# Post-LN attention and gated FFN on eight cores: statistics of the third layer norm taken chunk by chunk inside the w_d projection, its inputs loaded and cast earlier

## Chip, cores, metric

One Trainium2 chip, all 8 cores. Each core runs the same program on its own tokens; there is no exchange between cores. The metric is the time on the device, in microseconds, of the slowest core.

## The reference

What matters of it, for x of shape (4, 4096, 1024), 4 heads of 256:

```python
h = layer_norm(x, ln1_g, ln1_b)
q, k, v = heads(h @ wq), heads(h @ wk), heads(h @ wv)
attn = softmax(q*s, -1) @ (softmax(k*s, -2)^T v)       # linear attention
x1 = x + attn @ wo + bo
h = layer_norm(x1, ln2_g, ln2_b)
x2 = x1 + gelu(h @ w_ff1 + b_ff1) @ w_ff2 + b_ff2      # hidden 4096
u = x + (x2 @ w_d + b_d)                               # outer residual
x3 = layernorm(u)                                      # "ln3" in the kernel
z = (silu(x3 @ wg^T) * (x3 @ wu^T)) @ wd^T             # hidden 3072, weights /127
y = layernorm(x3 + z)                                  # "ln4" in the kernel
```

## The kernel before

Activations lie transposed: features on the 128 partitions in 8 chunks (`CH`), tokens along the free axis in tiles of 512 (`NT`). A core owns 2048 tokens, four tiles, and reads the other 2048 of its batch entry only for k and v. The program has two blocks, PA (ln1, k and v over 8 tiles, then q, then the small matrices of the attention) and PB (everything else). PB goes stage by stage over the four tiles: attention output, four quarters of the first FFN (`qq`, L807 on: 256 matmuls up with gelu on ACT, 256 matmuls down that DVE adds to the fp32 residual `R1`), then the stage of w_d (L943 to L987), then three rounds of the gated FFN (`r`, L1035 on), with ln4 and the output in the last.

Every engine carries out its instructions in the order in which `b.op` records them, and an instruction with a wait (`engine.wait_ge`, L84) holds all that is behind it on that engine. So the order of the Python code is the order of the work. `DmaQ` (L111) keeps two semaphores per queue: transfer k waits until transfer k-2 of the same queue has landed. `gpQ` is issued by POOL, `syQ` by SP.

The w_d stage, for each tile t:

- `est.acquire()` and `load_x` (L217) bring the tile of x, 2 MB, into a half of `estR` by SP. The first two of these wait for the last matmul of the first FFN (`q3b_done`).
- Eight ACT casts (L950) copy the fp32 tile of `R1` to bf16 `shad` (even t) or `shad2` (odd t, printed as shad_51). These lie in `Dr`, over the weights of the last up quarter, and so also wait for `q3a_done`.
- `rows()` and `bcs()` of the tile before (t-1): ACT and DVE turn the sums in PSUM bank `lnS` into mean and reciprocal deviation (L654 to L670), two matmuls spread them over 128 partitions (L676, L680).
- For each of eight output chunks m: eight matmuls (L963) with w_d in `slotD1`, and one DVE instruction (L973) that adds bias and x and writes `R1`. Three PSUM banks (`rot5`) rotate. w_d is loaded by POOL in four pieces of 256 columns (`gds`, L903), all of which wait for `q3b_done`; chunk m needs piece m//2.
- After m == 3, `l3_apply(t-1)`: eight DVE subtractions (L924), eight POOL products (L928) and eight ACT casts to `h2x` (L932).
- After the eight chunks, `stats()` of this tile: for each chunk an ACT cast to bf16 (L634), an ACT square (L636), and one matmul with a column of ones for each (L638, L642). The two buffers in `sbb` alternate between chunks, and all of it waits for the last L973 of the tile (`extra_stat_waits`).

The rows and the apply of tile 3 come in the first round of the gated FFN. `mk_ln` (L615) serves ln2 and ln4 too; there the statistics run on ACT, or on POOL where `cast_eng` is "gpsimd".

Of the kernel before, what the change touches and what calls it, by code (L numbers as in the profile page):

```python
# [125 lines left out]
def build_nc(debug=False, phases=99):  # L126
# [488 lines left out]
    def mk_ln(t, xsrc_c, kind, extra_stat_waits=(), cast_eng="scalar"):  # L615
# [6 lines left out]

        def stats():
            for c in range(CH):
                xb = sbb[:, (c % 2) * 512:(c % 2) * 512 + 512]
                xq_ = sbb[:, 1024 + (c % 2) * 512:1024 + (c % 2) * 512 + 512]
                vw = list(extra_stat_waits) + [("te", ln_state[f"sbb_free{c % 2}"])]
                if cast_eng == "gpsimd":
                    ve1 = b.op("gpsimd", lambda e, c=c, xb=xb: e.tensor_copy(
                        xb, xsrc_c(c)), waits=vw, inc="gp2")  # L630
                    ve2 = b.op("gpsimd", lambda e, xb=xb, xq_=xq_: e.tensor_mul(  # L631
                        xq_, xb, xb), inc="gp2")
                else:
                    ve1 = b.op("scalar", lambda e, c=c, xb=xb: e.activation(  # L634
                        xb, xsrc_c(c), AF.Identity), waits=vw, inc="se")
                    ve2 = b.op("scalar", lambda e, xb=xb, xq_=xq_: e.activation(  # L636
                        xq_, xb, AF.Square), inc="se")
                b.op("tensor", lambda e, xb=xb, c=c: e.matmul(  # L638
                    lnS["ap"][0:1, :], onescol, xb, start=(c == 0), stop=False,
                    skip_group_check=True),  # L640
                    waits=[(cast_sem, ve1)] + (Pool.w(lnS) if c == 0 else []))
                te = b.op("tensor", lambda e, xq_=xq_, c=c: e.matmul(  # L642
                    lnS["ap"][32:33, :], onescol, xq_, start=(c == 0), stop=False,
                    skip_group_check=True), waits=[(cast_sem, ve2)], inc="te")
# [554 lines left out]
```

How the kernel before makes its waits and increments, by code:

```python
        def run(engine, _w=tuple(w), _fn=fn, _s=semh, _k=inck):  # L82
            for sh, v in _w:
                engine.wait_ge(sh, v)
            inst = _fn(engine)
            if _s is not None:
                inst.then_inc(_s, _k)
# [38 lines left out]
def build_nc(debug=False, phases=99):  # L126
# [469 lines left out]
    def tap(name, src_handle, shape, dtype):  # L596
        th = nc.dram_tensor(name, shape, dtype, kind="ExternalOutput")
        b.begin("tap")
        ov = syQ.dma(lambda e: e.dma_start(th.ap(), src_handle[:, :]))
        b.op("sync", lambda e, ov=ov: e.wait_ge(b.sem[ov[0]], ov[1]))
        b.end()
# [517 lines left out]
                xsrc = lambda c, t=t: R1[:, c * NOWN + t * NT:  # L1119
                                         c * NOWN + (t + 1) * NT]
                L4[t] = mk_ln(t, xsrc, "ln4",
                              extra_stat_waits=[("ve", down_evac[t])])
                L4[t]["stats"]()
        wd_free[r % 2] = b.cnt["te"]
    L4[3]["rows"]()
    L4[3]["bcs"]()
    l4_apply(3)
    kf = syQ.k
    b.op("sync", lambda e, v=16 * ((kf + 1) // 2): e.wait_ge(b.sem["syA"], v))
    b.op("sync", lambda e, v=16 * (kf // 2): e.wait_ge(b.sem["syB"], v))
    b.end()
```

## Time and profile before

| | us |
|---|---|
| Time, median of 2 runs (2002.55 to 2003.36) | 2002.96 |
| The profiled execution's own time | 2016.04 |
| Its span on the slowest core, core 1 | 2014.5 |
| Spans of the eight cores | 1989.4 to 2014.5 |
| PE busy on core 1 | 1665.6 (83%) |
| DVE, ACT, POOL busy | 549.2, 517.9, 121.1 |

The time is that of the slowest core. All rows of the profile below are of core 1 in the one profiled execution; their times count from the start of its span. That execution took 13 us more than the median of the others. L-numbers are lines of the kernel before.

### The profile page before, as it was taken

The page shows a single profiled execution, that of the slowest core. Times are in us where ns is not written, and L with a number is a line of the kernel's source. Part 1 is how long each engine was busy: PE and PEld are TensorE (multiplying, and loading weights), DVE is VectorE, ACT ScalarE, POOL GpSimd, SP SyncE. Part 2 cuts the span into 40 slices and gives each one's busy share as a digit, 9 for nine tenths or more (in the row PEclk, how much of TensorE's full clock was granted, in tenths as well). Part 3 has the DMA queues.
Part 4 walks back from the last instruction along what each step waited for, and adds up shares of the span by engine and source line. Part 5 has one row for each costly group of instructions (what it writes and reads, how often), then busy time and mean ns, then how long its engine had stood idle before and what let it go on. Part 6 is the DMA issues. An engine that isn't in the chain of part 4 may idle for free.

```text
span 2014.5 us, 20572 instructions; the slowest of 8 cores (1989.4 to 2014.5 us)
## 1 busy us (share of the span) xinstructions
PE 1665.6 (83%) x7096; PEld 686.7 (34%) x7096; DVE 549.2 (27%) x840; ACT 517.9 (26%) x806; POOL 121.1 (6%) x124
## 2 busy tenths in 40 slices
PE   1489999898677767999999994567999999999774
PEld 0133333343222222444444441112344444444121
DVE  1633333311212442211213041222223213312223
ACT  1232333322232343122120312544210110011422
POOL 0000000000000042000000000111100000000113
PEclk9987777898797777999999997667899999999666
DMA  9311111020027050222211007101003003000112
GB/s 186 70 42 42 43 42 42 1 42 1 0 48 182 22 84 0 42 42 42 42 42 42 1 1 167 42 1 42 1 1 125 1 1 126 1 0 1 42 42 84
DMA packets 47636, 89.58 MB, mean 44 GB/s; under 512 B 1328, under 2 KB 5552, under 8 KB 47536
## 3 DMA queue, kind: packets, MB, share of 16 engines
q1 hardware_dynamic: 30896, 61.01, 9.3%
q0 software_dynamic: 16640, 27.26, 8.4%
q8 instruction: 60, 0.98, 0.2%
q14 instruction: 40, 0.33, 0.1%
HBM read 107.14 MB, written 8.39 MB: 57 GB/s over the span
## 4 chain that ended last, share of the span: by engine, by line
PE 50%; ACT 8%; DVE 4%; POOL 4%; DMA 3%; issue 2%; ACTq 0%; POOLq 0%; DVEq 0%; SPq 0%
PE pb L867 11%; PE pb L841 10%; PE pb L1051 8%; PE pb L1061 8%; PE pb L1104 8%; ACT sbb L636 3%; ACT sbb L634 3%; PE pb L769 2%; PE pb L963 2%; POOL R L928 2%; DMA estR<-xkv 2%; DMA slotD<-wdd 1%; DVE R L1013 1%; POOL sbb L631 1%; ACT shad L950 1%
## 5 line engine op out<-in xcount | busy, mean ns | idle before, releaser
L1051 PE MATMUL pb<-h2x,W 128*128 128x512 bf16 x768 | 186.1, 386 | 3.4 <-ACT slbt L1070 3.4
L1104 PE MATMUL pb<-Dr,wslotE 128*128 128x512 bf16 x768 | 177.0, 394 | 9.2 <-DVE R L1111 9.2
L1061 PE MATMUL pb<-h2x,W 128*128 128x512 bf16 x768 | 183.1, 381 | 0.0
L848 ACT ACTIVATE Gq<-pb,pv 128x512 bf16<-128x512 f32 x128 | 88.1, 689 | 312.0 <-PE pb L841 311.2
L1070 ACT ACTIVATE slbt<-pb 128x512 bf16<-128x512 f32 x96 | 57.4, 598 | 369.0 <-PE pb L1051 365.7
L1075 DVE SCALAR_TENSOR_TENSOR Dr<-slbt,pb 128x512 bf16<-128x512 bf16 x96 | 66.0, 688 | 287.4 <-PE pb L1061 260.0
L418 PE MATMUL pb<-W,h 128*128 128x512 bf16 x512 | 141.8, 428 | 0.0
L882 DVE TENSOR_TENSOR R<-R,pb 128x512 f32<-128x512 f32 x96 | 66.0, 688 | 265.5 <-PE pb L867 265.5
L434 PE MATMUL pb<-slotD,h 128*128 128x512 bf16 x512 | 135.9, 414 | 0.0
L841 PE MATMUL pb<-h2x,W 128*128 128x512 bf16 x512 | 121.0, 401 | 7.3 <-ACT Gq L848 6.0
L1104 PEld LDWEIGHTS pb<-Dr,wslotE 128*128 128x128 bf16 x768 | 76.9, 101 | 107.8 <-issue 23.6
L841 PE MATMUL pb<-h2x,slotD 128*128 128x512 bf16 x512 | 110.8, 379 | 0.0
L867 PE MATMUL pb<-Gq,slotD 128*128 128x512 bf16 x512 | 110.8, 379 | 0.0
L867 PE MATMUL pb<-Gq,W 128*128 128x512 bf16 x512 | 110.8, 379 | 0.0
L1051 PEld LDWEIGHTS pb<-h2x,W 128*128 128x128 bf16 x768 | 75.9, 99 | 97.5 <-issue 9.8
L1061 PEld LDWEIGHTS pb<-h2x,W 128*128 128x128 bf16 x768 | 75.7, 99 | 92.4 <-issue 3.2
L638 PE MATMUL pb<-sbb,cb 128*1 128x512 bf16 x96 | 53.4, 558 | 52.3 <-ACT sbb L634 32.3
L1111 DVE TENSOR_TENSOR R<-R,pb 128x512 f32<-128x512 f32 x96 | 66.0, 687 | 111.3 <-PE pb L1104 110.3
L963 PE MATMUL pb<-shad,slotD 128*128 128x512 bf16 x256 | 67.9, 431 | 29.0 <-DMA slotD<-wdd 19.8
L634 ACT ACTIVATE sbb<-R 128x512 bf16<-128x512 f32 x80 | 50.5, 631 | 155.4 <-DVE R L1111 77.3
L434 PEld LDWEIGHTS pb<-slotD,h 128*128 128x128 bf16 x512 | 53.6, 105 | 72.2 <-issue 48.2
L418 PEld LDWEIGHTS pb<-W,h 128*128 128x128 bf16 x512 | 52.9, 107 | 73.3 <-issue 52.9
(95 smaller groups left out, 1489.1 us busy)
## 6 DMA issues: line engine op xcount, KB each, us to landing
xq<-xkv SPq DMA_DIRECT2D x8, 2048.0 KB, 10.2
estR<-xkv SPq DMA_DIRECT2D x32, 256.0 KB, 3.1
W<-wff POOLq DMA_DIRECT2D x4, 2048.0 KB, 18.9
slotD<-wff POOLq DMA_DIRECT2D x4, 2048.0 KB, 16.4
estR<-xkv SPq DMA_DIRECT2D x4, 2048.0 KB, 11.5
y<-xq SPq DMA_DIRECT2D x4, 2048.0 KB, 6.9
W<-wgT SPq DMA_DIRECT2D x3, 2048.0 KB, 9.8
W<-wuT SPq DMA_DIRECT2D x3, 2048.0 KB, 15.2
```

Source lines behind the costliest of these rows:

```text
L418: b.op("tensor", lambda e, kc=kc, half=half, n0=n0, bk=bk: e.matmul(bk["ap"][:, :], h1[:, kc * N + n0: kc * N + n0 + 128], W1[:, kc * 1024 ...
L434: b.op("tensor", lambda e, kc=kc, half=half, n0=n0, bv=bv: e.matmul(bv["ap"][:, :], h1[:, kc * N + n0: kc * N + n0 + 128], slotD1[:, kc * ...
L634: ve1 = b.op("scalar", lambda e, c=c, xb=xb: e.activation(xb, xsrc_c(c), AF.Identity), waits=vw, inc="se")
L841: b.op("tensor", lambda e, jj=jj, kc=kc, t=t, s1=s1, bk=bk: e.matmul(bk["ap"][:, :], s1[:, kc * 1024 + jj * 128: kc * 1024 + (jj + 1) * 12 ...
L848: se = b.op("scalar", lambda e, jj=jj, t=t, qq=qq, bk=bk: e.activation(Gq[:, jj * NOWN + t * NT: jj * NOWN + (t + 1) * NT], bk["ap"][:, :] ...
L867: b.op("tensor", lambda e, m=m, jc=jc, t=t, s2=s2, bk=bk: e.matmul(bk["ap"][:, :], s2[:, jc * 1024 + m * 128: jc * 1024 + (m + 1) * 128], ...
L882: ve = b.op("vector", lambda e, m=m, t=t, bk=bk: e.tensor_add(R1[:, m * NOWN + t * NT: m * NOWN + (t + 1) * NT], R1[:, m * NOWN + t * NT: ...
L963: b.op("tensor", lambda e, m=m, kc=kc, bk=bk, sh=sh: e.matmul(bk["ap"][:, :], slotD1[:, kc * 1024 + m * 128: kc * 1024 + (m + 1) * 128], s ...
L1051: b.op("tensor", lambda e, hc=hc, kc=kc, t=t, bA=bA: e.matmul(bA["ap"][:, :], W0[:, kc * 1024 + hc * 128: kc * 1024 + (hc + 1) * 128], h2x ...
L1061: b.op("tensor", lambda e, hc=hc, kc=kc, t=t, bB=bB: e.matmul(bB["ap"][:, :], W1[:, kc * 1024 + hc * 128: kc * 1024 + (hc + 1) * 128], h2x ...
L1075: e.scalar_tensor_tensor(Ftn[:, hc * NOWN + t * NT: hc * NOWN + (t + 1) * NT], sl, S127, bB["ap"][:, :], ALU.mult, ALU.mult),
L1104: b.op("tensor", lambda e, m=m, hc=hc, t=t, wds=wds, bk=bk: e.matmul(bk["ap"][:, :], wds[:, hc * 1024 + m * 128: hc * 1024 + (m + 1) * 128 ...
```

## The change

Five edits.

1. In PA the load of wq is issued third instead of first, behind wk and wv.
2. The statistics of ln3 are no longer one block behind a tile. `stats_c(c)` handles one chunk. For tiles 0 to 2 it is recorded right behind the DVE instruction that writes this chunk of `R1`, and waits for it; for tile 3 all eight still stand behind the tile. The cast goes to POOL for even chunks, to ACT for chunks 1 and 5, to DVE for 3 and 7; the square is a DVE product of the bf16 copy with itself.
3. The bf16 copies of tiles 0 and 1 are made in the last down quarter of the first FFN, each chunk right after DVE has written it. Those of tiles 2 and 3 stay at the head of their tile.
4. Piece q of w_d waits for the last down matmul of tile 3 that reads its columns (chunk 2q+1), not for the end of the quarter.
5. `bcs(t-1)` moves from the head of the tile to before m == 2, `l3_apply(t-1)` from behind m == 3 to behind m == 4.

```diff
-    gq = load_w(W0, wq_d, D, CH)
     gk = load_w(W1, wk_d, D, CH)
     gv = load_w(slotD1, wv_d, D, CH)
+    gq = load_w(W0, wq_d, D, CH)
...
+        def stats_c(c, xw=()):
+            xb = sbb[:, (c % 2) * 512:(c % 2) * 512 + 512]
+            xq_ = sbb[:, 1024 + (c % 2) * 512:1024 + (c % 2) * 512 + 512]
+            vw = (list(extra_stat_waits) + list(xw)
+                  + [("te", ln_state[f"sbb_free{c % 2}"])])
+            if cast_eng == "p5":
+                ce = ("gpsimd" if c % 2 == 0
+                      else ("scalar" if c in (1, 5) else "vector"))
+            else:
+                ce = cast_eng
+            if ce == "gpsimd":
+                e1 = ("gp2", b.op("gpsimd", lambda e, c=c, xb=xb: e.tensor_copy(
+                    xb, xsrc_c(c)), waits=vw, inc="gp2"))
...
+            if cast_eng == "p5":
+                e2 = ("ve", b.op("vector", lambda e, xb=xb, xq_=xq_: e.tensor_mul(
+                    xq_, xb, xb), waits=[e1], inc="ve"))
...
+            b.op("tensor", lambda e, xb=xb, c=c: e.matmul(
+                lnS["ap"][0:1, :], onescol, xb, start=(c == 0), stop=False,
+                skip_group_check=True),
+                waits=[e1] + (Pool.w(lnS) if c == 0 else []))
+            te = b.op("tensor", lambda e, xq_=xq_, c=c: e.matmul(
+                lnS["ap"][32:33, :], onescol, xq_, start=(c == 0), stop=False,
+                skip_group_check=True), waits=[e2], inc="te")
...
                 if qq == 3:
                     r1_done[t] = b.cnt["ve"]
+                    if t < 2:
+                        sh_ = shad if t % 2 == 0 else shad2
+                        b.op("scalar", lambda e, m=m, t=t, sh_=sh_: e.activation(
+                            sh_[:, m * NT:(m + 1) * NT],
+                            R1[:, m * NOWN + t * NT: m * NOWN + (t + 1) * NT],
+                            AF.Identity),
+                            waits=[("ve", ve), ("te", q3a_done[0])], inc="se")
...
+                    if t == 3:
+                        q3b_m_te[m] = b.cnt["te"]
...
         ap3(wdd_d, q * 256, [[D, 128], [128 * D, CH], [1, 256]])),
-        waits=[("te", q3b_done[0])]) for q in range(4)]
+        waits=[("te", q3b_m_te[2 * q + 1])]) for q in range(4)]
...
+        L3.append(mk_ln(t, xsrc, "ln3", cast_eng="p5"))
+        if t >= 2:
...
         if t >= 1:
             L3[t - 1]["rows"]()
-            L3[t - 1]["bcs"]()
         for m in range(CH):
+            if m == 2 and t >= 1:
+                L3[t - 1]["bcs"]()
             bk = rot5.acquire()
...
             Pool.rel(bk, "ve", ve)
-            if m == 3 and t >= 1:
+            if t < 3:
+                L3[t]["stats_c"](m, xw=[("ve", ve)])
+            if m == 4 and t >= 1:
                 l3_apply(t - 1)
...
-        L3.append(mk_ln(t, xsrc, "ln3", extra_stat_waits=[("ve", u_evac[t])]))
-        L3[t]["stats"]()
+        if t == 3:
+            for c in range(CH):
+                L3[3]["stats_c"](c, xw=[("ve", u_evac[3])])
```

The order of PE's instructions around the start of tile 1 of the w_d stage, in the kernel before (slotD_49 holds w_d, sbb the statistics' operands, rowb the mean and deviation):

```order
L638 MATMUL pb<-sbb,cb 1x512
L642 MATMUL pb<-sbb,cb 1x512
L676 MATMUL pb<-rowb,cb 128x512
L680 MATMUL pb<-rowb,cb 128x512
L963 MATMUL pb<-shad_51,slotD_49 128x512 x64
L638 MATMUL pb<-sbb,cb 1x512
```

The same place now:

```order
L1002 MATMUL pb<-shad_51,slotD_49 128x512 x8
L651 MATMUL pb<-sbb,cb 1x512
L655 MATMUL pb<-sbb,cb 1x512
L1002 MATMUL pb<-shad_51,slotD_49 128x512 x8
L651 MATMUL pb<-sbb,cb 1x512
L655 MATMUL pb<-sbb,cb 1x512
L694 MATMUL pb<-rowb,cb 128x512
L698 MATMUL pb<-rowb,cb 128x512
L1002 MATMUL pb<-shad_51,slotD_49 128x512 x8
```

A tile's 64 matmuls stood together; now two statistics matmuls stand between every group of eight and the next, and the two spreading matmuls stand behind the second group.

ACT over tile 1 before (shad the bf16 copy of a tile, rsgb the spread deviation, h2x the normalised tile):

```order
L950 ACTIVATE shad_51<-R_43 128x512 x8
L654 ACTIVATE rowb<-pb 1x512
L667 ACTIVATE pb<-pb,pv 1x512
L670 ACTIVATE rowb<-pb 1x512
L919 ACTIVATE rsgb<-pb 128x512
L932 ACTIVATE h2x<-R_43 128x512 x8
L634 ACTIVATE sbb<-R_43 128x512
```

ACT over tile 1 now:

```order
L672 ACTIVATE rowb<-pb 1x512
L685 ACTIVATE pb<-pb,pv 1x512
L688 ACTIVATE rowb<-pb 1x512
L640 ACTIVATE sbb<-R_43 128x512
L951 ACTIVATE rsgb<-pb 128x512
L964 ACTIVATE h2x<-R_43 128x512 x8
L640 ACTIVATE sbb<-R_43 128x512
L985 ACTIVATE shad<-R_43 128x512 x8
```

The second L640 is the statistics cast of chunk 5; it stands behind the eight h2x casts of the tile before. The copy for tile 2 (L985) now stands ahead of the end of tile 1.

DVE in tile 1 now, from its fifth chunk on (R_43 is `R1`; L956 are the subtractions of the apply):

```order
L1012 SCALAR_TENSOR_TENSOR R_43<-pb,pv,estR 128x512
L643 TENSOR_TENSOR sbb<-sbb 128x512
L956 TENSOR_TENSOR R_43<-R_43,pb 128x512 x8
L1012 SCALAR_TENSOR_TENSOR R_43<-pb,pv,estR 128x512
L643 TENSOR_TENSOR sbb<-sbb 128x512
```

Before, it read

```order
L973 SCALAR_TENSOR_TENSOR R_43<-pb,pv,estR 128x512 x4
L924 TENSOR_TENSOR R_43<-R_43,pb 128x512 x8
L973 SCALAR_TENSOR_TENSOR R_43<-pb,pv,estR 128x512 x4
```

Each chunk's DVE instruction is now followed by the square of its chunk, and the subtractions stand one chunk later.

## Rows read from the trace of the kernel before

**Rows 1.** Busy time by window: w_d stage, tile 0's statistics; PEclk is the granted clock.

```profile
core 1: us, PE busy (x) PEld busy (x) DVE busy (x) ACT busy (x) POOL busy (x), PEclk, DMA share, GB/s
...
1207.82:1390.00 182.18, 107.19 (x327) 32.68 (x328) 45.33 (x63) 79.25 (x125) 31.29 (x28) 0.69 0.27 70
...
1243.10:1256.25 13.15, 8.70 (x16) 1.26 (x16) 0.75 (x1) 10.73 (x17) 0.00 (x0) 0.65 0.45 161
```

**Rows 2.** Timeline, start of PA: start, duration, engine, line, operation, idle time before.

```profile
26.52 0.88 POOL L223 DMA_DIRECT2D slotD<-wv  x1 [23.02 <-DMA W<-wq]
...
86.79 3.42 PE L418 MATMUL pb<-W,h 128*128 128x512 bf16 x8
```

**Rows 3.** DMA issues: count, size each, median us from issue to landing.

```profile
slotD<-wv POOLq DMA_DIRECT2D x1, 2048.0 KB, 34.1
```

**Rows 4.** Timeline, start of the w_d stage.

```profile
1207.94 81.49 SPq L217 DMA_DIRECT2D estR<-xkv  x4
...
1208.41 1.75 POOL L903 DMA_DIRECT2D slotD<-wdd  x2 [220.14 <-PE pb L867]
1227.35 4.89 PE L963 MATMUL pb<-shad,slotD 128*128 128x512 bf16 x16 [19.54 <-DMA slotD<-wdd]
...
1230.69 0.75 DVE L973 SCALAR_TENSOR_TENSOR R<-pb,pv,estR 128x512 f32<-128x512 f32 x1 [22.02 <-PE pb L963]
```

**Rows 5.** Issue to landing of L217's loads: at 1205 to 1240 us, then all.

```profile
DMA to landing us min/median/max: 14.4/18.4/22.4
DMA to landing us min/median/max: 8.6/10.2/47.8
```

**Rows 6.** Timeline, from the end of tile 0 to the start of tile 1.

```profile
1244.04 0.63 ACT L634 ACTIVATE sbb<-R 128x512 bf16<-128x512 f32 x1 [70.97 <-DVE R L973]
...
1244.82 0.38 PE L638 MATMUL pb<-sbb,cb 128*1 128x512 bf16 x1 [1.85 <-ACT sbb L634]
...
1255.62 5.69 ACT L950 ACTIVATE shad<-R 128x512 bf16<-128x512 f32 x8
...
1266.92 0.58 PE L680 MATMUL pb<-rowb,cb 1*128 1x512 bf16 x1 [4.21 <-ACT rowb L670]
1267.43 13.97 PE L963 MATMUL pb<-shad,slotD 128*128 128x512 bf16 x56
```

**Rows 7.** Timeline, the apply of tile 0 within tile 1.

```profile
1277.25 6.23 DVE L924 TENSOR_TENSOR R<-R,pb 128x512 f32<-128x512 f32 x8
1278.09 10.25 POOL L928 TENSOR_TENSOR R<-R,rsgb 128x512 f32<-128x512 f32 x8 [44.36 <-DVE R L924]
...
1284.49 3.52 PE L963 MATMUL pb<-shad,slotD 128*128 128x512 bf16 x8 [3.09 <-DVE R L973]
...
1288.18 0.75 DVE L973 SCALAR_TENSOR_TENSOR R<-pb,pv,estR 128x512 f32<-128x512 f32 x1 [2.13 <-PE pb L963]
1288.49 0.63 ACT L932 ACTIVATE h2x<-R 128x512 bf16<-128x512 f32 x1 [0.67 <-POOL R L928]
```

**Rows 8.** Duration min/median/max in ns, first and last start, by line.

```profile
L330 DVE CAST sbb<-xq x64: 426/427/428, 32.6 to 367.1; 128x512 bf16<-128x512 f32 x64
L397 DVE TENSOR_SCALAR h<-h,pv x64: 352/353/355, 55.7 to 408.9; 128x512 bf16<-128x512 bf16 x64
L629 POOL CAST sbb<-R x16: 609/610/630, 707.1 to 766.0; 128x512 bf16<-128x512 f32 x16
```

**Rows 9.** Timeline in PA: a statistics matmul, a group of eight, its ACT reader.

```profile
105.33 0.38 PE L339 MATMUL pb<-sbb,cb 128*1 128x512 bf16 x1 [0.22 <-ACT sbb L332]
105.63 1.90 PE L418 MATMUL pb<-W,h 128*128 128x512 bf16 x8
...
107.69 0.60 ACT L426 ACTIVATE ebf<-pb 128x512 bf16<-128x512 f32 x1 [2.50 <-PE pb L418]
```

**Rows 10.** Timeline, the first statistics cast of tile 3.

```profile
1377.62 0.63 ACT L634 ACTIVATE sbb<-R 128x512 bf16<-128x512 f32 x1
```

**Rows 11.** Chain that ended last: start, us, what; first matmuls of the gated FFN.

```profile
1389.83 3.53 PE pb L1051 x8
```

More of the change, by code:

```diff
@@ L623, in stats @@
         def stats():
             for c in range(CH):
[L625 to L644, printed above, removed]
@@ L645, in stats @@
-                ln_state[f"sbb_free{c % 2}"] = te
-            ch["stat_done"] = b.cnt["te"]
+                stats_c(c)
         def rows():
@@ L687, in mk_ln @@
         ch["stats"] = stats
+        ch["stats_c"] = stats_c
         ch["rows"] = rows
@@ L803, in build_nc @@
     r1_done = [0, 0, 0, 0]
+    shv01 = [0, 0]
+    q3b_m_te = [0] * CH
     q2_done = [0, 0]
@@ L947, in build_nc @@
         syv = load_x(th, toff, t * NT, waits=Pool.w(slot))
-        shv = 0
-        for c in range(CH):
-            shv = b.op("scalar", lambda e, c=c, t=t, sh=sh: e.activation(
-                sh[:, c * NT:(c + 1) * NT],
-                R1[:, c * NOWN + t * NT: c * NOWN + (t + 1) * NT], AF.Identity),
-                waits=[("te", shad_free[t % 2]), ("ve", r1_done[t]),
-                       ("te", q3a_done[0])], inc="se")
+        xsrc = lambda c, t=t: R1[:, c * NOWN + t * NT: c * NOWN + (t + 1) * NT]
+        L3.append(mk_ln(t, xsrc, "ln3", cast_eng="p5"))
+        if t >= 2:
+            shv = 0
+            for c in range(CH):
+                shv = b.op("scalar", lambda e, c=c, t=t, sh=sh: e.activation(
+                    sh[:, c * NT:(c + 1) * NT],
+                    R1[:, c * NOWN + t * NT: c * NOWN + (t + 1) * NT],
+                    AF.Identity),
+                    waits=[("te", shad_free[t % 2]), ("ve", r1_done[t])],
+                    inc="se")
+        else:
+            shv = shv01[t]
         if t >= 1:
             L3[t - 1]["rows"]()
-            L3[t - 1]["bcs"]()
         for m in range(CH):
+            if m == 2 and t >= 1:
+                L3[t - 1]["bcs"]()
             bk = rot5.acquire()
@@ L982, in build_nc @@
         Pool.rel(slot, "ve", u_evac[t])
-        xsrc = lambda c, t=t: R1[:, c * NOWN + t * NT: c * NOWN + (t + 1) * NT]
-        L3.append(mk_ln(t, xsrc, "ln3", extra_stat_waits=[("ve", u_evac[t])]))
-        L3[t]["stats"]()
+        if t == 3:
+            for c in range(CH):
+                L3[3]["stats_c"](c, xw=[("ve", u_evac[3])])
     u_all = b.cnt["ve"]
```

17 lines of the change are left out of this document (added).

## Prediction

> **What bounds the kernel now.** I first read the windows by stage. In most stages PE runs without a gap. The w_d stage is one of the few where it does not: 182.2 us from 1207.82 to 1390.00, of which PE is busy 107.2, at a granted share of the clock of 0.69 [rows 1]. Four of the five edits aim at this stage, so I followed its timeline from the first matmul to the first one of the gated FFN, and noted at each gap of PE who ended it.
>
> There are four kinds of gap. (a) At the start PE waits 19.5 us for w_d [rows 4]. (b) Behind a tile, ACT makes the statistics alone: from 1244.04 to 1255.62, 11.6 us for eight chunks; PE only follows. (c) Then come eight bf16 copies (5.69 us) and the rows, and PE takes up the next tile only at 1267.43 [rows 6]. So between the last chunk of tile 0 and the next group of matmuls lie about 24 us. (d) In the middle of a tile the eight subtractions on DVE hold up the eviction of PSUM, and PE waits 3.09 us [rows 7]. A tile costs 44 us in which its 64 matmuls need 14. Outside this stage the change hardly acts.
>
> A row to watch for: in the statistics of tile 0 the granted clock is 0.65 [rows 1], and eight matmuls after them take 3.4 to 3.5 us [rows 2, 7] where eight at full clock take 1.90 [rows 9]. Those are the two levels, 1.2 and 2.4 GHz.
>
> **Edit 1, the order of the first loads.** The third load of this queue is issued at 26.52, when the first has landed [rows 2], and takes 34.1 us [rows 3], so all three are there at 60.6. PE reads wk first at 86.79 [rows 2], behind the layer norms of two tiles, which need x and no weight. So 26 us of slack cover the order, and the bytes moved are the same. Price 0; I allow 1 us either way for how they share the DMA engines with x.
>
> **Edit 4 and the start.** Piece 0 of w_d now waits for the second of the eight chunks of the last down tile, some 10 us earlier (six groups at 1.73), while the DMA engines are idle. Pieces 0 and 1 should be there when the quarter ends at 1207.8, so PE's wait for w_d goes. What is late next is x: both loads are issued at 1207.94 as before [rows 4], and the first eviction adds x. They took 14.4 and 22.4 us to land beside two pieces of w_d; a load of the same size takes 8.6 in the best case [rows 5]. Now part of the w_d traffic is gone and pieces 2 and 3 still overlap. I take the middle, 11.5 (ends 8.6 and 14.4): the first eviction starts at 1219.4, where it started at 1230.69. That is 11.3 us gained.
>
> **Edit 2, the period of a chunk.** This is what decides. In tiles 0 to 2, PE has behind each group of eight matmuls the two statistics matmuls of the same chunk, and its next group is queued behind them. They need eviction, cast and square of this very chunk, so nothing overlaps. One period at full clock:
>
> - group start to eviction start 2.06 (105.63 to 107.69) [rows 9]
> - eviction 0.75 [rows 4]
> - hand-over 0.15 (a cast that ends at 1244.67, PE at 1244.82) [rows 6]
> - cast 0.61 on POOL [rows 8], 0.63 on ACT [rows 6]
> - hand-over 0.15, square on DVE 0.43, hand-over 0.15
> - statistics matmul to next group 0.30 (105.33 to 105.63) [rows 9]
>
> Together 4.60 us. At half clock the first term is 3.69 (1284.49 to 1288.18) [rows 7] and the last 0.51 (1266.92 to 1267.43) [rows 6]: 6.44 us. No row has a DVE product of two bf16 tensors in SBUF. Its bounds are the bf16 TENSOR_SCALAR at 0.35 [rows 8] and the fp32 TENSOR_TENSOR, at most 0.78 by its spacing (8 in 6.23) [rows 7]; I take the cast from fp32, 0.43 [rows 8], being nearest in bytes read. Over 24 periods the ends are worth -2 and +8 us. Two casts of eight are on DVE at 0.43 instead, worth 1 us less in all, which I leave out.
>
> The VectorE page of the Trainium skill (VectorE: DVE Perf Modes, "The perf-mode tier table") gives bf16 `tensor_tensor` in SBUF the same rate as an fp32 copy; no run here shows it, and by it the square would also be about 0.43.
>
> Which clock? After an idle stretch of 3.09 us eight matmuls ran at half clock (3.52) [rows 7]; statistics alone pulled it down to 0.65 on average [rows 1]. The new pattern has, at full clock, a burst of about 1.9 us and some 2.6 us with one short matmul in it; at half clock the burst is 3.5 of 6.4. The first should lose the clock often, the second regain it often. I take the middle: P = 5.5 us. Three tiles then cost 44 us each for the chunks alone, and nothing behind them.
>
> **Edits 3 and 5.** The copies of tiles 0 and 1 go to the last down quarter, where ACT has nothing else in its order, one of 0.7 us per 1.73 us of PE: price 0 there, and the 5.69 us between tiles 0 and 1 [rows 6] go. Those of tiles 2 and 3 now stand on ACT ahead of the last two chunks of the tile before: 5.7 us under two periods of 11. The rows run beside m = 0 and 1, and PE pays two short matmuls, 1.0 us. If that cover were gone it would be the 5 us of the rows chain per tile.
>
> The apply gets dearer. Chunk 5's cast stands on ACT behind eight h2x casts, which follow POOL. From the first subtraction to the last h2x cast starting are 11.24 us (1277.25 to 1288.49) [rows 7], so the cast of chunk 5 starts 11.95 after it. Add cast, two hand-overs, square, hand-over and 0.51: 13.8, less the 0.4 by which group 5 starts after the subtraction: 13.4 us for this period, in tiles 1 and 2.
>
> **The sum**, from the end of the first FFN at 1207.8, with P = 5.5:
>
> - tile 0: eviction at 1219.4; chunk 0 through at 1222.2 (0.75 + 0.15 + 0.61 + 0.15 + 0.43 + 0.15 + 0.51 = 2.75); seven more periods, 38.5: 1260.7
> - tiles 1 and 2: seven periods 38.5, chunk 5 13.4, spreading 1.0, so 52.9 each: 1313.6 and 1366.5
> - tile 3: from its first group to the first subtraction 9.8 before (1267.43 to 1277.25) [rows 6, 7]; now one group (1.7) and the spreading (1.0) more: 12.5, at 1379.0. POOL is free 0.84 + 10.25 later [rows 7]: 1390.1. Before, the first cast was at 1377.62 [rows 10].
> - its statistics: two chunks at a time, each pair one cast, square, matmul and three hand-overs, 2.0 us; ACT joins at 1391.0. With four pairs the last is through at 1399.0, and the gated FFN starts at 1399.3. These take 9.2 where they took 12.2 (1377.62 to 1389.83) [rows 10, 11].
>
> Before, it started at 1389.83 [rows 11]. So 9.5 us are lost in all: 11 won at the start, about 24 won behind each of three tiles, 3 on the last statistics, and more than that given back in 21 periods which cost 5.5 instead of 1.73, and in the two long ones. The profiled execution would come to 2016.04 + 9.5 = 2025.5; it stands 13.1 over the median of the runs, and the stage is bound by engines, not by what differs between executions, so the median comes to 2002.96 + 9.5 = 2012.5. A measurement of this kernel can tell about 2% (40 us) from no change, so this is within it.
>
> **Rivals.** Each period weighs 21 times, so the outcome hangs on P.
>
> - A, the forecast: P about 5.5, time 2012.5. Chance 0.5.
> - B, PE stays at half clock: P = 6.44, 21 x 0.94 = 19.7 more, 2032. For it: every group after a pause in this stage started at half clock [rows 7]. [...] Chance 0.17. The Trainium skill (TensorE: Matmul & The Clock Gate, "HAM oscillation — how this bites in real kernels") says that bursts shorter than the waits between them find the array at half clock each time. By that rule this rival is the case; the 3.09 us gap agrees.
> - C, not slower: PE keeps the full clock, because two statistics matmuls break the gap. P = 4.60, 21 x 0.9 = 18.9 less, 1993.6. It decides from P = 5.05 down (9.5 / 21 = 0.45 under 5.5). For it: in PA, where bursts and statistics alternate, groups right behind statistics ran at full clock (1.90) [rows 9]. Against: gaps there were shorter. Chance 0.23.
> - D, the early w_d load buys less than it should: x lands no earlier than before (14.4), and pieces 2 and 3 come late beside it, so that m = 4 and 6 wait. 2.9 + about 3 more, 2018. Chance 0.1.
>
> **Numbers.** 2012.5. The range reaches from C to B, both ends rounded by the unknown square: 1993 to 2034. Faster by over 2% would be under 1963, which no case comes near: 0.02. Slower by over 2% is over 2043; B with the dear square comes close: 0.05. Within: 0.93.
>
> **What would show it.** In the changed profile: the first w_d group starting at the end of the down quarter, and its first eviction ended by the DMA of x at about 1219; 24 groups of eight matmuls, each followed by a PE wait released by DVE (the square), with a period of 5.5; a wait of over 8 us before the statistics of chunk 5 of tiles 1 and 2, released by ACT; the gated FFN starting about 1399. The start of PA unchanged to a microsecond. I am wrong if the period is under 5 or over 6.3, if PE does not wait for each chunk's statistics, or if ACT's cast of chunk 5 is not the long one.

## The result, and the profile after

| | before | after |
|---|---|---|
| Median of the runs, us | 2002.27 (8 runs, 2001.05 to 2004.01) | 2022.31 (9 runs, 2018.25 to 2268.39) |
| The profiled execution's own time | 2016.04 | 2020.53 |
| Its span on the slowest core | 2014.5 (core 1) | 2018.9 (core 3) |
| w_d stage, median of eight cores | 182.1 | 205.1 |
| gated FFN, median of eight cores | 623.5 | 621.8 |

The changed kernel takes 1.0095 of the time before (95% interval 1.0083 to 1.0107), 19 us more by the ratio and 20 by the medians. The forecast was 2012.5, 9.5 us more, with a range of 1993 to 2034 and 0.93 for "within 2%". The sign and the verdict came as forecast; the loss is twice the forecast.

Here and below, the w_d stage runs from the last matmul of the first FFN to the first of the gated FFN, as the timeline of each core gives it, and "the stage" is the median over the eight cores. The ratios leave out executions in which a die ran slower (three of these nine, from 2111.93 us), but some that they keep have a pair of cores that took some 20 to 25 us more in a stage that no edit touches, so an experiment's theory is judged by the w_d stage, and its whole time only where a ratio is given.

All the other stages stand still. The first matmul of k comes at 86.6 us (86.9 before; medians of the eight cores), the attention takes 120.0 (119.7), the first FFN 501.6 (501.6). The stage brings +23.0 and the gated FFN gives back 1.7. That is 21, and the runs say 19 to 20.

The page of the changed kernel, core 3: the granted clock over the span in 40 slices, and the groups of the statistics matmuls and of the w_d matmuls, whose last numbers are the idle time of PE just before them and what ended most of it.

```profile
PEclk9998888998887768999999987568899999999766
...
L651 PE MATMUL pb<-sbb,cb 128*1 128x512 bf16 x96 | 51.2, 535 | 123.5 <-ACT sbb L640 50.8
...
L1002 PE MATMUL pb<-shad,slotD 128*128 128x512 bf16 x256 | 90.1, 521 | 0.0
```

The groups of w_d wait for nothing (0.0), and the statistics matmuls (all layer norms of this helper together) wait 123.5 us. So the statistics stand on the path, not the products. ACT is named for 50.8 of it, but only half of that lies in the w_d stage. The list of waits of the stage alone (waiting for, total us, count, longest):

```profile
PE pb L651 <- POOL sbb L634: 37.9, 13, 16.3
...
PE pb L651 <- ACT sbb L640: 25.0, 6, 8.9
```

The 25.0 us for ACT are two long waits for chunk 5 (8.64 and 8.90) and four of about 1.9. Of the 37.9 us for POOL, 16.3 are the first wait, in which POOL itself waits for the eviction that needs x.

The windows of the whole stage and of the seven regular periods of tile 0:

```profile
core 3: us, PE busy (x) PEld busy (x) DVE busy (x) ACT busy (x) POOL busy (x), PEclk, DMA share, GB/s
1190.40:1396.01 205.61, 121.08 (x327) 34.43 (x324) 62.36 (x103) 38.85 (x61) 38.44 (x41) 0.68 0.17 46
1209.57:1249.39 39.82, 25.62 (x72) 7.51 (x71) 9.09 (x16) 1.26 (x2) 1.84 (x3) 0.79 0.04 13
```

The first row answers to [rows 1]. ACT has lost half of its work (79.3 to 38.9) and DVE took some (45.3 to 62.4). PE runs the same number of matmuls, but they take 121.1 us instead of 107.2, since more of them run at half clock. The second row says what a period costs: 39.82 / 7 = 5.69 us.

The timeline from the start of the stage into the period (start, duration, engine, line, operation, idle time before and its releaser):

```profile
1180.65 0.88 POOL L935 DMA_DIRECT2D slotD<-wdd  x1 [209.78 <-PE pb L888]
...
1190.24 1.89 PE L1002 MATMUL pb<-shad,slotD 128*128 128x512 bf16 x8
1190.54 0.99 SPq L217 DMA_DIRECT2D estR<-xkv  x2
...
1192.11 0.89 POOL L935 DMA_DIRECT2D slotD<-wdd  x1 [3.67 <-DMA slotD<-wdd]
...
1206.81 0.75 DVE L1012 SCALAR_TENSOR_TENSOR R<-pb,pv,estR 128x512 f32<-128x512 f32 x1 [15.54 <-DMA estR<-xkv]
...
1209.57 3.39 PE L1002 MATMUL pb<-shad,slotD 128*128 128x512 bf16 x8
...
1215.72 3.32 PE L1002 MATMUL pb<-shad,slotD 128*128 128x512 bf16 x8
...
1219.21 0.75 DVE L1012 SCALAR_TENSOR_TENSOR R<-pb,pv,estR 128x512 f32<-128x512 f32 x1 [3.95 <-PE pb L1002]
1220.22 0.61 POOL L634 CAST sbb<-R 128x512 bf16<-128x512 f32 x1 [11.91 <-DVE R L1012]
...
1220.97 0.38 PE L651 MATMUL pb<-sbb,cb 128*1 128x512 bf16 x1 [1.94 <-POOL sbb L634]
1221.00 0.43 DVE L643 TENSOR_TENSOR sbb<-sbb 128x512 bf16<-128x512 bf16 x1 [1.04 <-POOL sbb L634]
...
1221.57 0.38 PE L655 MATMUL pb<-sbb,cb 128*1 128x512 bf16 x1 [0.22 <-DVE sbb L643]
...
1221.88 1.90 PE L1002 MATMUL pb<-shad,slotD 128*128 128x512 bf16 x8
```

The reader sees the closed loop. A group of w_d ends, DVE evicts it, POOL casts, PE takes the sum of the copy, DVE squares, PE takes the sum of the squares, and only then does the next group start, though the last of its operands, piece 1 of w_d, landed at 1191.58. The first groups run at half clock (3.39 and 3.32 for eight) and the one at 1221.88 at full clock (1.90).

The apply in tile 1, which answers to [rows 7]:

```profile
1282.17 6.23 DVE L956 TENSOR_TENSOR R<-R,pb 128x512 f32<-128x512 f32 x8
...
1282.73 3.60 PE L1002 MATMUL pb<-shad,slotD 128*128 128x512 bf16 x8
...
1283.07 10.25 POOL L960 TENSOR_TENSOR R<-R,rsgb 128x512 f32<-128x512 f32 x8 [1.60 <-DVE R L956]
...
1293.46 0.63 ACT L964 ACTIVATE h2x<-R 128x512 bf16<-128x512 f32 x1 [0.67 <-POOL R L960]
1294.18 0.63 ACT L640 ACTIVATE sbb<-R 128x512 bf16<-128x512 f32 x1
...
1294.96 0.59 PE L651 MATMUL pb<-sbb,cb 128*1 128x512 bf16 x1 [8.64 <-ACT sbb L640]
...
1296.07 2.81 PE L1002 MATMUL pb<-shad,slotD 128*128 128x512 bf16 x8
```

ACT makes the cast of chunk 5 at 1294.18, behind the last h2x cast, and PE waits 8.64 us for it: this period takes 1296.07 - 1282.73 = 13.34 us.

The end of the stage: the first statistics cast of tile 3, and the first group of the gated FFN, which answers to [rows 10, 11].

```profile
1386.88 0.61 POOL L634 CAST sbb<-R 128x512 bf16<-128x512 f32 x1
...
1396.01 1.90 PE L1092 MATMUL pb<-h2x,W 128*128 128x512 bf16 x8
```

This group now runs at full clock (1.90) where the first one of before took 3.53 [rows 11]. The statistics matmuls ahead of it are closer together than they were (16 in 8.3 us, 11.4 before). It is tempting to see in this the 1.7 us that the gated FFN gives back, but the runs don't bear it out: with chunk 5's cast on DVE (below) the first group also takes 1.90 us on every core, and the gated FFN takes 624.0. Where the 1.7 us come from stays open.

### The profile page after: what moved, and what is told of

Its sections match the earlier page's. It is cut to its first block, busy times and chain, and to the rows that moved or that the text cites. A ratio compares the mean times of both kernels' runs of the same rounds, so it can differ in the third digit from the quotient of the medians.

```text
span 2018.9 us, 20608 instructions; the slowest of 8 cores (2009.3 to 2018.9 us)
## 1 busy us (share of the span) xinstructions
PE 1650.2 (82%) x7096; PEld 680.4 (34%) x7096; DVE 566.3 (28%) x880; ACT 482.6 (24%) x750; POOL 130.8 (6%) x140
## 4 chain that ended last, share of the span: by engine, by line
PE 52%; DVE 5%; DMA 4%; POOL 4%; ACT 4%; issue 2%; DVEq 0%; POOLq 0%; ACTq 0%; SPq 0%
PE pb L888 11%; PE pb L862 10%; PE pb L1092 8%; PE pb L1102 8%; PE pb L1145 8%; DMA estR<-xkv 4%; PE pb L1002 4%; POOL R L960 2%; ACT sbb L640 1%; ACT sbb L649 1%; POOL sbb L634 1%; DVE R L1012 1%; DVE R L1054 1%; PE pb L655 1%; POOL sbb L646 1%
## 5 line engine op out<-in xcount | busy, mean ns | idle before, releaser
L651 PE MATMUL pb<-sbb,cb 128*1 128x512 bf16 x96 | 51.2, 535 | 123.5 <-ACT sbb L640 50.8
L418 PE MATMUL pb<-W,h 128*128 128x512 bf16 x512 | 128.5, 396 | 0.4 <-ACT ebf L426 0.4
L434 PE MATMUL pb<-slotD,h 128*128 128x512 bf16 x512 | 122.7, 383 | 0.0
L1145 PEld LDWEIGHTS pb<-Dr,wslotE 128*128 128x128 bf16 x768 | 76.8, 101 | 107.2 <-issue 22.9
L1092 PEld LDWEIGHTS pb<-h2x,W 128*128 128x128 bf16 x768 | 75.6, 99 | 96.4 <-issue 7.9
L1102 PEld LDWEIGHTS pb<-h2x,W 128*128 128x128 bf16 x768 | 75.7, 99 | 92.6 <-issue 3.5
L1002 PE MATMUL pb<-shad,slotD 128*128 128x512 bf16 x256 | 90.1, 521 | 0.0
L334 PE MATMUL pb<-sbb,cb 128*1 128x512 bf16 x64 | 35.1, 549 | 59.3 <-DVE sbb L330 58.7
L862 PEld LDWEIGHTS pb<-h2x,W 128*128 128x128 bf16 x512 | 52.0, 103 | 75.7 <-issue 22.2
L788 PE MATMUL pb<-Q,CW 128*128 128x512 bf16 x256 | 64.3, 414 | 14.5 <-DVE R L796 13.2
## 6 DMA issues: line engine op xcount, KB each, us to landing
xq<-xkv SPq DMA_DIRECT2D x8, 2048.0 KB, 10.9
estR<-xkv SPq DMA_DIRECT2D x4, 2048.0 KB, 12.5
```

Of the source, the lines that this page charges most:

```text
L418: b.op("tensor", lambda e, kc=kc, half=half, n0=n0, bk=bk: e.matmul(bk["ap"][:, :], h1[:, kc * N + n0: kc * N + n0 + 128], W1[:, kc * 1024 ...
L434: b.op("tensor", lambda e, kc=kc, half=half, n0=n0, bv=bv: e.matmul(bv["ap"][:, :], h1[:, kc * N + n0: kc * N + n0 + 128], slotD1[:, kc * ...
L862: b.op("tensor", lambda e, jj=jj, kc=kc, t=t, s1=s1, bk=bk: e.matmul(bk["ap"][:, :], s1[:, kc * 1024 + jj * 128: kc * 1024 + (jj + 1) * 12 ...
L1002: b.op("tensor", lambda e, m=m, kc=kc, bk=bk, sh=sh: e.matmul(bk["ap"][:, :], slotD1[:, kc * 1024 + m * 128: kc * 1024 + (m + 1) * 128], s ...
L1092: b.op("tensor", lambda e, hc=hc, kc=kc, t=t, bA=bA: e.matmul(bA["ap"][:, :], W0[:, kc * 1024 + hc * 128: kc * 1024 + (hc + 1) * 128], h2x ...
L1102: b.op("tensor", lambda e, hc=hc, kc=kc, t=t, bB=bB: e.matmul(bB["ap"][:, :], W1[:, kc * 1024 + hc * 128: kc * 1024 + (hc + 1) * 128], h2x ...
```

## Experiments

In each diff, + and - are against the changed kernel. Its own stage is 205.1 us.

### Which edits cost, which pay: edit 2 undone

The statistics go back behind the tile, on ACT. The other four edits stay.

```diff
-        L3.append(mk_ln(t, xsrc, "ln3", cast_eng="p5"))
+        L3.append(mk_ln(t, xsrc, "ln3"))
...
-            if t < 3:
-                L3[t]["stats_c"](m, xw=[("ve", ve)])
...
-        if t == 3:
-            for c in range(CH):
-                L3[3]["stats_c"](c, xw=[("ve", u_evac[3])])
+        for c in range(CH):
+            L3[t]["stats_c"](c, xw=[("ve", u_evac[t])])
```

> Edit 2 alone is undone: the statistics of ln3 stand behind the tile again, all on ACT, 11.6 us a tile; edits 1, 3, 4, 5 stay. Theory 1 (the serial chunk period on PE is what costs; edits 3 to 5 do bring what was forecast): the w_d stage falls from the 205 us of the changed kernel to about 162 (eviction of x 16.4 after the down quarter, 25 for tile 0, then some 36, 42 and 42), so the time is about 1980, 20 us under the kernel before. Rival (the loss is elsewhere, and edits 3 to 5 bring nothing): about 2002 like the kernel before, or over 2010.

Measured: stage 161.3 us, ratio to before 0.9947 (0.9902 to 0.9993). The timeline shows the open loop, on core 4: the first three evictions in a row, and the first statistics cast only behind the tile.

```profile
1202.03 2.46 DVE L1012 SCALAR_TENSOR_TENSOR R<-pb,pv,estR 128x512 f32<-128x512 f32 x3 [15.64 <-DMA estR<-xkv]
...
1215.08 0.63 ACT L640 ACTIVATE sbb<-R 128x512 bf16<-128x512 f32 x1 [55.55 <-DVE R L1012]
```

It follows that edits 3 to 5 are worth 182.1 - 161.3 = 21 us by themselves, and that edit 2 costs 205.1 - 161.3 = 44. The change as a whole is slower because of this edit alone. Edits 3 and 5 were not undone one by one.

### Is it the clock: the pause filled

Eight more matmuls behind each group of tiles 0 to 2 go into a free PSUM bank. Nothing is left out; their result isn't used.

```diff
             if t < 3:
+                for kc in range(CH):
+                    w = Pool.w(bst[3]) if kc == 0 else []
+                    b.op("tensor", lambda e, m=m, kc=kc, sh=sh: e.matmul(
+                        pbs[3][:, :],
+                        slotD1[:, kc * 1024 + m * 128: kc * 1024 + (m + 1) * 128],
+                        sh[:, kc * NT:(kc + 1) * NT],
+                        start=(kc == 0), stop=(kc == 7)), waits=w,
+                        inc="te" if kc == 7 else None)
+                if m == CH - 1:
+                    shad_free[t % 2] = b.cnt["te"]
                 L3[t]["stats_c"](m, xw=[("ve", ve)])
```

> The changed kernel with eight extra matmuls into an unused PSUM bank behind each chunk's group in tiles 0 to 2; they fit into the wait of PE at full clock and only keep it busy. Theory 2 (0.5 us and more of each period comes from the clock that PE loses in its waits): the period falls from 6.0 to about 4.65, 21 periods, some 25 us less, about 1997. Rival (the period is set by hand-overs and the engines' durations alone, the clock is no matter): no gain, 2022 or more, since the extra matmuls cost up to 3 us a period at half clock.

Measured: stage 181.0, ratio 0.999 (0.9959 to 1.0021). One period on core 1 (L1021 are the added matmuls), and a window of core 5:

```profile
1217.50 1.90 PE L1002 MATMUL pb<-shad,slotD 128*128 128x512 bf16 x8
1219.24 1.89 PE L1021 MATMUL pb<-shad,slotD 128*128 128x512 bf16 x8
...
1221.34 0.38 PE L651 MATMUL pb<-sbb,cb 128*1 128x512 bf16 x1 [0.21 <-POOL sbb L634]
...
1222.24 1.90 PE L1002 MATMUL pb<-shad,slotD 128*128 128x512 bf16 x8
```

```profile
1215.00:1235.00 20.00, 18.63 (x79) 7.04 (x77) 5.81 (x10) 0.63 (x1) 1.75 (x3) 1.00 0.00 1
```

The granted clock is 1.00 and the period 1222.24 - 1217.50 = 4.74 us with a POOL cast, which the forecast had at 4.60. The added work hides wholly in the wait and holds PE at its upper level through tile 0. It doesn't do so everywhere: from 1274.00 to 1280.50, in the long period of chunk 5, the granted clock on core 5 is 0.50. So 24 us of the changed kernel's stage hang on the clock, and what stays above edit 2 undone is 20 us. This isn't an exact split of the 44, since the stage with edit 2 undone also runs at a granted clock of only 0.72.

### Chunk 5 behind ACT's queue

```diff
-                      else ("scalar" if c in (1, 5) else "vector"))
+                      else ("scalar" if c == 1 else "vector"))
```

> The changed kernel with the statistics cast of chunk 5 on DVE instead of ACT. Theory 3 (chunk 5's cast waits behind the eight h2x casts of the apply, which follow POOL): the period of chunk 5 in tiles 1 and 2 falls from 13.4 to about 8.5, which is the subtractions on DVE plus the chain; about 10 us less, 2012. Rival (PE waits there for the DVE eviction behind the subtractions anyway): no change, 2022.

Measured: stage 195.3, ratio 1.0052 (1.0036 to 1.0068). The period of chunk 5 on core 2:

```profile
1281.80 6.23 DVE L956 TENSOR_TENSOR R<-R,pb 128x512 f32<-128x512 f32 x8
1288.13 0.75 DVE L1012 SCALAR_TENSOR_TENSOR R<-pb,pv,estR 128x512 f32<-128x512 f32 x1
1288.99 0.43 DVE L637 CAST sbb<-R 128x512 bf16<-128x512 f32 x1
...
1289.56 0.59 PE L651 MATMUL pb<-sbb,cb 128*1 128x512 bf16 x1 [4.60 <-DVE sbb L637]
...
1291.37 3.59 PE L1002 MATMUL pb<-shad,slotD 128*128 128x512 bf16 x8
```

The period falls from 13.3 to 9.2 us, and PE's wait from 8.64 to 4.60. What is late next is DVE: the eviction stands behind the eight subtractions. Two long periods make 8 of the 9.8 us. One changed condition moves a cast to another queue, and that is worth half of the whole loss.

### Opening the loop: statistics two chunks later, on all engines

```diff
-            if t < 3:
-                L3[t]["stats_c"](m, xw=[("ve", ve)])
+            evs.append(ve)
+            if t < 3 and m >= 2:
+                L3[t]["stats_c"](m - 2, xw=[("ve", evs[m - 2])])
...
+        if t < 3:
+            for c in (6, 7):
+                L3[t]["stats_c"](c, xw=[("ve", evs[c])])
```

> The changed kernel with the statistics of chunk m recorded two chunks later (behind the DVE instruction of chunk m+2; chunks 6 and 7 behind the tile), on all engines; the same instructions otherwise. Theory 1 (what costs is that PE's next group is queued behind statistics that need the chunk just computed): the chunk period falls towards 2.3 us, only the stall by the apply stays (about 11 us in tiles 1 and 2), the stage takes about 130 us instead of 205, the time is about 1945 to 1960. Rival (DVE, POOL and ACT together set the period): over 2000.

Measured: stage 150.3, ratio 0.9847 (0.983 to 0.9865). It beats the kernel before by 1.5%, but the expected stage is missed by 20 us. Core 6:

```profile
1209.98 3.59 PE L1003 MATMUL pb<-shad,slotD 128*128 128x512 bf16 x8
1213.50 0.58 PE L651 MATMUL pb<-sbb,cb 128*1 128x512 bf16 x1
1213.75 0.75 DVE L1013 SCALAR_TENSOR_TENSOR R<-pb,pv,estR 128x512 f32<-128x512 f32 x1 [4.43 <-PE pb L1003]
1214.60 0.42 DVE L643 TENSOR_TENSOR sbb<-sbb 128x512 bf16<-128x512 bf16 x1
...
1215.17 0.59 PE L655 MATMUL pb<-sbb,cb 128*1 128x512 bf16 x1 [1.09 <-DVE sbb L643]
1215.69 3.23 PE L1003 MATMUL pb<-shad,slotD 128*128 128x512 bf16 x8
```

The sum of the copy no longer waits. But the square of chunk m-2 is recorded behind the eviction of chunk m on DVE, and PE's next group stands behind the sum of that square. The loop is shorter (two engines instead of three) and still closed: 1215.69 - 1209.98 = 5.7 us here, at half clock, and 3.8 at full clock (core 0, groups at 1210.55 and 1214.37). From the first eviction of tile 0 to the eighth it takes 24.4 us, 3.5 per chunk (41.2 and 5.9 in the changed kernel); the 5.3 for tile 0 in the next expectation is a period at half clock, not the mean.

### The same delay on PE alone

Casts and squares stay right behind the eviction of their chunk; only the two matmuls are recorded later, behind the group of chunk m+2 and ahead of its eviction.

```diff
+            if defer:
+                ch["pend"].append((c, xb, xq_, e1, e2))
+            else:
+                stats_pe(c, xb, xq_, e1, e2)
...
+        def stats_pe(c, xb, xq_, e1, e2):
             b.op("tensor", lambda e, xb=xb, c=c: e.matmul(
...
+            if t < 3 and m >= 2:
+                L3[t]["flush"]()
             ve = b.op(
...
-                L3[t]["stats_c"](m, xw=[("ve", ve)])
+                L3[t]["stats_c"](m, xw=[("ve", ve)], defer=True)
...
+        if t < 3:
+            L3[t]["flush"](2)
```

> The changed kernel with only PE's two statistics matmuls of chunk m moved: they stand behind the matmuls of group m+2 (those of 6 and 7 behind the tile); casts and squares stay right behind the eviction. In lag2, which moved casts and squares too, the square of chunk m stood on DVE behind the eviction of m+2, so that PE still waited once per chunk (period about 5.3 in tile 0, stage 150). Theory 1, sharpened (the loop PE group, eviction, square, PE statistics is closed once per chunk in both): without it the period falls to 2.3 to 2.6, the stage to about 132 (33 for tile 0, 28 and 32 for tiles 1 and 2, 38 for tile 3), the time to about 1952. Rival (DVE, which waits for POOL's cast before each square, sets the period): the period stays at 3 or more and the stage over 150, 1970.

Measured: stage 135.1 (132 expected), ratio 0.9748 (0.9732 to 0.9763), median 1950.20 (1952 expected). Core 1:

```profile
1215.73 1.90 PE L1017 MATMUL pb<-shad,slotD 128*128 128x512 bf16 x8
1217.56 0.38 PE L666 MATMUL pb<-sbb,cb 128*1 128x512 bf16 x1
1217.57 0.38 PE L670 MATMUL pb<-sbb,cb 128*1 128x512 bf16 x1
1217.88 1.90 PE L1017 MATMUL pb<-shad,slotD 128*128 128x512 bf16 x8
...
1220.02 1.90 PE L1017 MATMUL pb<-shad,slotD 128*128 128x512 bf16 x8
```

A period is 2.14 us, at full clock, with no wait in it. The same instructions as in the changed kernel, in another order on one engine, are worth 70 us. This settles the theory: what cost the time was the place of two matmuls in PE's queue, not the work of the statistics. It also turns edit 2 from a loss into a gain: with the statistics behind the tile the stage was 161.3.

### Why x lands late: the traffic beside it

First, pieces 2 and 3 of w_d wait until x of tile 0 has landed; then, the x of tile 1 waits for it instead.

```diff
+    x0e = load_x(estR, 0, 0, waits=[("te", q3b_done[0])])
...
-        waits=[("te", q3b_m_te[2 * q + 1])]) for q in range(4)]
+        waits=[("te", q3b_m_te[2 * q + 1])] + ([x0e] if q >= 2 else []))
+        for q in range(4)]
...
-        syv = load_x(th, toff, t * NT, waits=Pool.w(slot))
+        syv = x0e if t == 0 else load_x(th, toff, t * NT, waits=Pool.w(slot))
```

> The changed kernel with pieces 2 and 3 of w_d waiting until the first tile of x has landed; nothing else moves. Theory 4 (the first eviction comes 16.4 us after the down quarter instead of the 11.6 forecast since w_d pieces still run beside x): x lands 4 to 5 us earlier, stage 205 to about 200.5, time about 2017. Rival (the load of the second tile, issued at once behind it, or the latency itself): no change, 2021.

```diff
-        syv = load_x(th, toff, t * NT, waits=Pool.w(slot))
+        syv = load_x(th, toff, t * NT,
+                     waits=Pool.w(slot) + ([x0e[0]] if t == 1 else []))
+        if t == 0:
+            x0e = [syv]
```

> The changed kernel with the load of x for tile 1 waiting until that for tile 0 has landed. If the two loads share the engines, the first eviction comes up to 4 us earlier (about 2017); if the first goes ahead anyway and w_d is what shares with it, nothing changes (2021). My theory 4 says the latter.

Measured, from the end of the first FFN to the first eviction: 17.0 us in the changed kernel, 12.6 with w_d held back, 15.1 with the second x held back. So w_d beside it costs x 4.4 us. The other x costs 1.9 by the same sum, but that is close to the scatter: in the runs that leave these loads as they are, the median runs from 16.0 (edit 1 undone) to 17.2 us, and single cores from under 15 to nearly 19. Neither brings much in the end. The stages are 202.3 and 205.0 and the ratios 1.0091 both (1.0073 to 1.0109 and 1.0075 to 1.0107). Of the 4.4 us, tile 0 loses 1.4 again (48.2 us instead of 46.8 from its first eviction to that of tile 1), as it does with the second x held back; the cores of one run differ by more than that.

### Edit 1 undone, edit 4 undone

```diff
+    gq = load_w(W0, wq_d, D, CH)
     gk = load_w(W1, wk_d, D, CH)
     gv = load_w(slotD1, wv_d, D, CH)
-    gq = load_w(W0, wq_d, D, CH)
```

> The changed kernel with edit 1 undone: wq is loaded first again. My step (26 us of slack cover the order): start to first k matmul stays at 86 us, the time at about 2021. Rival (the order does move the first matmuls, or the DMA engines' sharing with x): a few us either way in the first stage.

```diff
-        waits=[("te", q3b_m_te[2 * q + 1])]) for q in range(4)]
+        waits=[("te", q3b_done[0])]) for q in range(4)]
```

> The changed kernel with edit 4 undone: all four pieces of w_d wait for the end of the down quarter again. If the early load is what brought the first eviction from 23 to 17 us behind that end, it goes back to 20 to 23 and the stage to about 209, time about 2025. Rival (x alone sets the first eviction): 17, no change.

Measured for edit 1: first matmul of k at 86.9 us (86.6 with the edit), stage 204.5. The ratio is 1.0122 (1.008 to 1.0164), and this interval holds the changed kernel's 1.0095. So no effect is to be seen. For edit 4: first eviction 23.3 us after the end of the first FFN instead of 17.0, stage 214.6. So edit 4 is worth 9.5 us. 6.3 of them are the first eviction; the other 3 lie in tile 0 (50.7 us instead of 46.8 from its first eviction to that of tile 1), in which, behind its first group, PE waits for no DMA. The version has no ratio; its shortest execution took 2027.76 us, where 2025 was expected.

### A version that beats both

It joins what paid: the delayed matmuls, w_d behind x, the cast of chunk 5 on DVE. Added are these: the last two statistics of a tile flushed into the next tile; rows before m == 2 and bcs before m == 4; the apply spread, two chunks behind each of m = 4 to 7; and the bf16 copies of tiles 2 and 3 made one per chunk in the tile before.

```diff
+            if t >= 1 and m < 2:
+                L3[t - 1]["flush"]()
...
-            if m == 4 and t >= 1:
-                l3_apply(t - 1)
+            if t in (1, 2):
+                nt, nsh = t + 1, (shad if t % 2 == 1 else shad2)
+                shv01[nt] = b.op("scalar", lambda e, m=m, nt=nt, nsh=nsh: e.activation(
+                    nsh[:, m * NT:(m + 1) * NT],
+                    R1[:, m * NOWN + nt * NT: m * NOWN + (nt + 1) * NT],
+                    AF.Identity),
+                    waits=[("te", shad_free[nt % 2]), ("ve", r1_done[nt])],
+                    inc="se")
+            if m >= 4 and t >= 1:
+                l3_apply(t - 1, 2 * (m - 4), 2 * (m - 4) + 2)
```

> lagpe and xfirst together, and: the last two statistics of a tile on PE stand behind the first two groups of the next tile, rows at m = 2 and spreading at m = 4 there; the bf16 copies of tiles 2 and 3 one per chunk in the tile before; the apply spread, two chunks behind each of m = 4 to 7; chunk 5's cast on DVE. If the three causes found (serial chunk period, apply in one block, x beside w_d) are all there is, the stage comes to about 113 us (29, 26, 26, 32) and the time to about 1933, under both kernels. Rival (DVE becomes the bound of every tile): 125 to 135, 1950.

Measured: stage 130.1, ratio 0.9714 (0.9693 to 0.9734), median 1943.39. It is the fastest of all, 57 us under the kernel before by its ratio. But 113 us were expected for the stage, and 130.1 lies where the rival put it (125 to 135). The rival's reason isn't shown by that: DVE is busy for 66.9 of the 126.8 us of core 0's stage. The list of waits in the stage of core 0 names one of the waits behind it:

```profile
PE pb L1012 <- ACT shad L1036: 18.1, 2, 9.3
```

The first group of tiles 2 and 3 waits for the last bf16 copy of its tile, which ACT makes behind h2x casts that follow POOL. It is the fault of chunk 5 once more, made by me. The last run moves these copies to m = 0 to 3, two each (the diff is against the version above).

```diff
-            if t in (1, 2):
+            for c in {0: (0, 1), 1: (2, 3), 2: (4, 5), 3: (6, 7)}.get(m, ()):
+                if t not in (1, 2):
+                    break
```

> best with the bf16 copies of tiles 2 and 3 two per chunk behind m = 0 to 3, ahead of the apply's casts on ACT. In best PE waited 17.9 us in two pieces at the head of tiles 2 and 3 for the last copy, which stood on ACT behind casts that wait for POOL. If that is the cause, tiles 1 and 2 fall from 32.5 to about 24 us each, the stage from 130 to about 114, the time to about 1928. Rival (PE would wait there for DVE or the statistics anyway): 1940.

Measured: stage 128.8, where 114 was expected. The version has no ratio; its four executions took 1952.29 to 2017.92 us, and 1928 was expected. The list of waits in the stage of core 0:

```profile
DVE sbb L643 <- POOL sbb L634: 21.8, 16, 3.3
...
PE pb L666 <- POOL sbb L634: 11.5, 4, 7.5
PE pb L666 <- ACT h2x L984: 10.1, 2, 8.0
```

The wait for the copies is gone and others have come, as the rival said: statistics casts on POOL, which now stand behind the products of the apply, and PE's statistics behind them. It looks as if POOL's queue held the tile now, with its eight products of 1.28 us and four casts, but POOL is busy for only 39.3 of the 129.4 us of this stage, and no run shows it.

## Why the prediction was right, and where it was off

The frame held: the stage decides, PE loses the loop of edit 2, the gains at the start and behind the tiles don't cover it, and the result is slower by less than 2%. Step by step, for the profiled core (from 1190.4 to 1396.01, 205.6 us, against 182.0 before: +23.6, forecast +9.5):

- **Edit 1: price 0.** Right, by the undone edit.
- **Edit 4 and the start.** The w_d wait went, as forecast, and x was late next. The size was off. I gave x 11.5 us to land, and the first eviction came at 1206.81, 16.4 us after the end of the quarter instead of 11.6: +4.8. That pieces 2 and 3 still overlap was in the text, but I took the middle between two rows. The runs show that the overlap is what counts (12.6 without it). The part of rival D on x was nearest, and it went past D's end of 14.4. Its late pieces, which should have cost 3 us, didn't appear.
- **Edit 2, the period.** The parts of the sum are right to a few hundredths but for one. The square took 0.42 to 0.43 us, as long as the cast from fp32 on DVE (0.43); the table of the Trainium skill (VectorE: DVE Perf Modes, "The perf-mode tier table") gives both the same rate, and the trace agrees. The exception is the hand-over to POOL: the eviction of 1219.21 ends at 1219.96 and the cast starts at 1220.22, 0.26 us later instead of 0.15. The periods at full clock were 4.75 with a POOL cast (forecast 4.60) and 4.34 with a DVE cast. At half clock they were 6.6 (forecast 6.44). The term that was mis-sized is the middle: with P = 5.5 between 4.60 and 6.44, I gave PE half of its periods at full clock. In tile 0 the mean was 5.69, in tiles 1 and 2, without chunk 5 and the spreading, 6.28 and 6.09: +1.3, +5.4 and +4.1 for these tiles. In tile 0 of core 3 two groups took 1.90 us, the others 3.2 to 3.6. Of the 16 groups of tiles 1 and 2 none took less than 2.7. Four of them began at full clock and lost it on the way, five began at half clock and got the full one on the way, and seven ran at half clock throughout. In the windows of core 3 the granted clock stands last but two: a group's first 0.4 us, and then 47.7 us with five whole groups.

```profile
1249.39:1249.79 0.40, 0.40 (x3) 0.20 (x3) 0.00 (x0) 0.18 (x1) 0.00 (x0) 1.00 0.00 0
1250.20:1297.90 47.70, 29.36 (x65) 7.43 (x63) 14.36 (x23) 12.05 (x19) 11.09 (x11) 0.50 0.14 44
```

- **Rivals B and C.** Neither came. The mean period of the 21, 6.02, lies about midway between A's 5.5 and B's 6.44, and so does the time (2022 between 2012.5 and 2032). B let no group have the full clock; over the eight cores 59 of the 184 groups from chunk 1 of tile 0 to the end of tile 2 began with it, as the length of their first matmul shows (0.39 us, not 0.61). The rule of the Trainium skill beside B (TensorE: Matmul & The Clock Gate, "HAM oscillation — how this bites in real kernels"), that such bursts find half clock each time, thus fits 125 of the 184 and differs in the rest. Two of the reasons given for B were misread. The 3.09 us gap that was said to agree with the rule stands behind 14 us of matmuls, which is no burst shorter than its wait. And not every group after a pause began at half clock: in tile 2 of the kernel before, the one behind the same pause began at full clock (granted 1.00 from 1328.50 to 1328.90) and lost it on the way.

```profile
1328.48 3.14 PE L963 MATMUL pb<-shad,slotD 128*128 128x512 bf16 x8 [3.09 <-DVE R L973]
```

C fell, and the filled pause shows what C's condition would have brought: a period of 4.74, a stage 24 us shorter, and no loss (ratio 0.999).
- **Chunk 5: 13.4 us.** Right: 13.34 in tile 1 and 13.45 in tile 2. The working names one hand-over too many for its 13.8: from cast to next group there are two, and with them its terms give it. That moving one cast cures a third of this period, I didn't say.
- **Tile 3 and the end.** From its first group to the first subtraction it took 10.9 us (1364.71 to 1375.60), 1.6 less than the 12.5 forecast: I had charged an extra group at half clock, and PE was faster here. Its statistics took 9.13 (forecast 9.2).

The differences add up: 4.8 + 1.3 + 5.4 + 4.1 - 1.6 = 14.0, and 9.5 + 14.0 = 23.5 against the measured 23.6. The gated FFN then returns 1.7, which the forecast didn't have. The range, 1993 to 2034, held a gain as well as a loss, so it proves little that the time lies in it; what the runs bear out are the steps.

What stays open is why the alternation falls as it does. It isn't a matter of the tile: on core 3 no group of tiles 1 and 2 took 1.90 us, but on five of the other cores one or two did, and over all cores 21 of 56 groups began at full clock in tile 0 and 38 of 128 in tiles 1 and 2. No run tells more.
